# A language-model tower on one core: two rank-eight products per tile moved into two 32-row strips of the matmul array

## The chip, the cores and the metric

The kernel runs on one core of a Trainium2 chip. The time is the device time of one execution in microseconds (us), lower being better. TensorE does the matrix products (the profile calls its products PE and its weight loads PEld), VectorE is DVE, ScalarE is ACT, GpSimd is POOL and SyncE is SP.

## The reference

The input is 16 sequences of 1024 token ids. For each position the 16 latest embeddings (64 wide) are joined, multiplied by `w1` and passed through tanh; `w2` makes 1024 logits of the 64 values.

```
h = jnp.tanh(x @ w1 + b1);  logits = h @ w2 + b2
h = h + attn(layernorm(h))          # autocorrelation, top 6 lags, softmax, weighted roll
h = h + ffn(layernorm(h))           # x @ W.T + bias + sum over 16 experts of a rank-16 update
```

`attn` takes the circular autocorrelation of each row of length 1024 and adds up the row rolled by the six best lags with softmax weights; where lag 0 outweighs all others by far, it returns its input. The kernel has a short way for that case and a general one behind a flag; in the runs here the short way is taken.

## The kernel before

On the short way each output row is a sum of few matrix products of the 64 tanh values with fixed matrices. A row of `out` is `a * (product) + mean`, where `a` and `mean` are numbers per position. The product has a large part, 128 rows deep (64 rows for `h` against the centred `w2`, 64 for `beta * h` against the FFN's matrix), and a small part of rank eight: bias rows times the constants 1, beta and 1/a of each position.

Values are kept as float32r in a high and a low half. So a tile of 128 positions and 1024 outputs, in two halves `n` of 512, takes for each half three full products (`u_hi` by `w_hi`, `u_lo` by `w_hi`, `u_hi` by `w_lo`) and a fourth for the rank-eight part: `xT` by `extra`. The eight bias rows stand in `extra[i]` at partitions 32 i to 32 i + 7, with zeros elsewhere; `xT` holds the eight constants of four tiles at partitions 0, 32, 64 and 96, so the zeros of `extra[i % 4]` pick out the tile. All four products are 128 rows deep. They add up in one of the four banks of `o_ps`; two tiles fit. ScalarE evicts the first half of a tile (line 500), VectorE the second (line 676), and SP stores pairs of tiles.

A sequence has eight tiles. The work is a software pipeline over steps, one sequence per step and stage: `front` gathers the embeddings (GpSimd, `gather_rows`), transposes them and does the convolution with `w1` in two halves (lines 989 and 992); `mid` transposes the tanh values, takes moments (line 1096), computes the variances (VectorE, line 773 to 808), a chain of seven operations on GpSimd (lines 436 to 448, from `var_eps` to `beta`), and on VectorE `bh_row` in `u_rows` (line 783) and `x_row` (lines 785 to 792); `back` does the eight tile products. The orders on each engine are written out by hand. On TensorE a step is: tile 0; transposes of `h` and moments; transposes of the gathered rows; tile 1; moments; tiles 2 and 3; convolution half 0; tiles 4 and 5; a wait for `u_ready`; transposes of `u_rows` (line 1147) and, behind a wait for `x_ready`, two of `x_row` (line 1153); convolution half 1; tiles 6 and 7. ScalarE copies the transposed `x_row` to `xT` (line 574).

The rows of `extra` are made once: GpSimd fills the four tiles with zeros in step 1, behind `acf_done` (line 431), since two of them held a table before; SP then writes the eight rows into `extra[0]` (lines 344 and 347) and copies them into the other three at their partitions (line 350). TensorE waits for the first set behind step 1 and for the copies (`rows_in`) at tile 1 of step 2, the first step with tiles.

Names that the rows show: `moments` and `hbar` belong to the set-up, where lines 981 to 984 and 997 do small products with 65 rows and, at line 984, with one row (partition 64).

Of the kernel before, what the change touches and what calls it, by code (L numbers as in the profile page):

```python
# [67 lines left out]
def tower_kernel(nc, ids, wte, w1, b1, w2, b2, wT, bias, aT, bfT, coeffs, scales,  # L68
                 ident, dft, idft, acf, lags, out, force_general=False):
    ctx = ExitStack()  # L70
    with ctx:
        def sb(name, shape, dt=F32):
            return ctx.enter_context(nc.sbuf_tensor(name, shape, dt))
# [21 lines left out]
        last_moments = sb("last_moments", [P, 3])  # L95
        w_hi = sb("w_hi", [P, L], F32R)
        w_lo = sb("w_lo", [P, L], F32R)
        extra = [sb(f"extra{i}", [P, L], F32R) for i in range(4)]
        aT_sb = sb("aT_sb", [P, KC, ER])
        bfT_sb = sb("bfT_sb", [P, 2, L])  # L100
        bias_row = sb("bias_row", [1, L])
# [9 lines left out]
        hT = [sb(f"hT{p}", [P, T]) for p in range(2)]  # L111
        u_hi = [sb(f"u_hi{p}", [P, T], F32R) for p in range(2)]
        u_lo = [sb(f"u_lo{p}", [P, T], F32R) for p in range(2)]
        xT = [sb(f"xT{p}", [P, 2 * P], F32R) for p in range(2)]
        a_sb = [sb(f"a_sb{p}", [P, NT]) for p in range(2)]
        mean_sb = [sb(f"mean_sb{p}", [P, NT]) for p in range(2)]

# [3 lines left out]
        h_row = u_rows[:, 0:NT * (E + 1)].rearrange("p (i n) -> p i n", i=NT)  # L121
        bh_row = u_rows[:, NT * (E + 1):].rearrange("p (i e) -> p i e", i=NT)
        odd = sb("odd", [P, T + 1])
        x_row = sb("x_row", [P, NT, XW], F32R)
        prod = sb("prod", [P, NT, E + 1])
        quad = sb("quad", [P, NT])
        var = sb("var", [P, NT])
# [98 lines left out]
        xa_kept = sem("xa_kept")  # L226
        g_done = sem("g_done")
        w_hi_set = sem("w_hi_set")
        extra_zeroed = sem("extra_zeroed")
        w_set = sem("w_set")  # L230
        g_hi_set = sem("g_hi_set")
        row0_in, rows_in = sem("row0_in"), sem("rows_in")
# [75 lines left out]
        def _(sp):  # L308
# [29 lines left out]
            load_wT(1)  # L338
            sp.dma_start(bfT_sb[:, :, :], bfT.rearrange("(c p) n -> p c n", p=P)).then_inc(bfT_in, 16)

            sp.wait_ge(extra_zeroed, 1)
            sp.wait_ge(w_set, 3)
            for n, row in ((0, b_hi), (1, b_lo), (5, bias_hi), (6, bias_lo), (7, bias_hi)):
                sp.dma_start(extra[0][n:n + 1, :].bitcast(F32), row.bitcast(F32)).then_inc(row0_in, 16)
# [2 lines left out]
                sp.dma_start(extra[0][n:n + 1, :].bitcast(F32), row.bitcast(F32)).then_inc(row0_in, 16)  # L347
            sp.wait_ge(row0_in, 16 * NX)
            for i in range(1, 4):
                sp.dma_start(extra[i][XW * i:XW * i + NX, :].bitcast(F32), extra[0][0:NX, :].bitcast(F32)).then_inc(rows_in, 16)  # L350

            def step(g, u, front, mid, back):
                if back:
# [41 lines left out]
        def _(pool):  # L395
# [13 lines left out]
            gather(0, 0, 0)  # L409
            for i in range(NT):  # L410
                gather_rows(0, i)
            pool.memset(x_row[:, :, :].bitcast(F32), 0.0)
            pool.memset(minus_half[:, :], -0.5)
            pool.memset(g_ones[:, :], 1.0)
            pool.memset(cert_max[:, :], -3.0e38)
            pool.memset(h_row[:, :, E:E + 1], 2.0).then_inc(zeros_set, 1)
            pool.wait_ge(zeros_set, 1)
            pool.memset(x_row[:, :, 0:2].bitcast(F32), 1.0).then_inc(zeros_set, 1)

            def step(g, u, front, mid, back, last=False):  # L420
                a, b = 2 * g + u, 2 * g + u - 1
                more = front and not last
                if more:

                    gather(a + 1, 1 - u, a)
                    for i in range(NT // 2):
                        gather_rows(1 - u, i)
                if in_step(1, g, u):
                    pool.wait_ge(acf_done, 1)
                    for i in range(4):  # L430
                        last_fill = pool.memset(extra[i][:, :].bitcast(F32), 0.0)
                    last_fill.then_inc(extra_zeroed, 1)
                if mid:
                    pb = 1 - u
                    wait_alone(pool, var_ready, b + 1, pool_passed)
                    pool.tensor_scalar(var_eps[:, :], var[:, :], EPS, None, ALU.add).then_inc(scal_step, 1)  # L436
                    wait_alone(pool, scal_step, 7 * b + 1, pool_passed)
                    pool.tensor_tensor(inv_std[:, :], var_eps[:, :], minus_half[:, :], ALU.pow).then_inc(scal_step, 1)  # L438
                    wait_alone(pool, scal_step, 7 * b + 2, pool_passed)
                    pool.tensor_scalar(a_sb[pb][:, :], inv_std[:, :], 1.0, None, ALU.add).then_inc(scal_step, 1)  # L440
                    wait_alone(pool, scal_step, 7 * b + 3, pool_passed)
                    pool.tensor_tensor(a_sq[:, :], a_sb[pb][:, :], a_sb[pb][:, :], ALU.mult).then_inc(scal_step, 1)
                    wait_alone(pool, scal_step, 7 * b + 4, pool_passed)
                    pool.tensor_tensor(var2[:, :], a_sq[:, :], var[:, :], ALU.mult).then_inc(scal_step, 1)
                    wait_alone(pool, scal_step, 7 * b + 5, pool_passed)
                    pool.tensor_scalar(var2_eps[:, :], var2[:, :], EPS, None, ALU.add).then_inc(scal_step, 1)  # L446
                    wait_alone(pool, scal_step, 7 * b + 6, pool_passed)
                    pool.tensor_tensor(beta[:, :], var2_eps[:, :], minus_half[:, :], ALU.pow).then_inc(scal_step, 1)  # L448
                    if in_step(1, g, u):
                        pool.wait_ge(g_done, 1)  # L450
                    pool.wait_ge(h_ready, b + 1)
                    pool.tensor_copy(h_all[:, bass.ds(NT * E * b, NT * E)].rearrange("p (i e) -> p i e", i=NT),
                                     h_row[:, :, 0:E]).then_inc(h_saved, 1)
                if more:
                    for i in range(NT // 2, NT):
                        gather_rows(1 - u, i)
# [25 lines left out]
        def _(act):  # L482
# [20 lines left out]
            def step(g, u, front, mid, back):  # L503
# [65 lines left out]
                if mid:  # L569
                    act.wait_ge(ut_done, b + 1)  # L570
                    for odd_tiles in range(2):
                        nc.scalar.copy(tiles_of(u_hi[pb][E:P, :], odd_tiles), pair_bank(sum_ps, odd_tiles)).then_inc(hi_kept, 1)
                    act.wait_ge(xt_done, b + 1)
                    nc.scalar.copy(xT[pb][:, :], et_ps[:, 0:2 * P]).then_inc(xt_kept, 1)
                if front:
                    keep_odd(1)
                if front:
# [41 lines left out]
        def _(dve):  # L619
# [121 lines left out]
            def step(g, u, front, mid, back):  # L741
# [25 lines left out]
                def variance(hh):  # L767
# [9 lines left out]
                    dve.wait_ge(prod_ready, 2 * b + hh + 1)  # L777
                    nc.vector.tensor_reduce(in_pairs(quad[:, :])[:, pairs], products, AX.X, ALU.add).then_inc(quad_ready, 1)

                def scale_h():  # L780

                    dve.wait_ge(scal_step, 7 * b + 7)
                    nc.vector.tensor_tensor(bh_row, h_row[:, :, 0:E],  # L783
                                            beta[:, :].unsqueeze(2).to_broadcast([P, NT, E]), ALU.mult).then_inc(u_ready, 1)
                    nc.vector.reciprocal(inv_a[:, :], a_sb[pb][:, :]).then_inc(x_step, 1)
                    nc.vector.tensor_copy(x_row[:, :, 2:4], beta[:, :].unsqueeze(2).to_broadcast([P, NT, 2])).then_inc(x_step, 1)
                    dve.wait_ge(x_step, 3 * b + 1)
                    nc.vector.tensor_copy(x_row[:, :, 5:7], inv_a[:, :].unsqueeze(2).to_broadcast([P, NT, 2])).then_inc(x_step, 1)
                    dve.wait_ge(x_step, 3 * b + 2)
                    nc.vector.tensor_tensor(x_row[:, :, 4], beta[:, :], x_row[:, :, 2].bitcast(F32), ALU.subtract)  # L790
                    dve.wait_ge(x_step, 3 * b + 3)
                    nc.vector.tensor_tensor(x_row[:, :, 7], inv_a[:, :], x_row[:, :, 5].bitcast(F32),
                                            ALU.subtract).then_inc(x_ready, 1)

                if back:
# [167 lines left out]
        def _(pe):  # L963
# [78 lines left out]
            def step(g, u, front, mid, back):  # L1042
# [3 lines left out]
                def tile_product(i):  # L1046

                    if i == 0:
                        pe.wait_ge(h_hi_kept, c + 1)
                        pe.wait_ge(h_lo_kept, c + 1)  # L1050
                        pe.wait_ge(hi_kept, 2 * c + 2)
                        pe.wait_ge(lo_kept, 2 * c + 2)
                        pe.wait_ge(xt_kept, c + 1)
                    if i == 1 and in_step(2, g, u):
                        pe.wait_ge(rows_in, 48)

                    ge(pe, oa_kept, NT * c + i - 1)
                    ge(pe, ov_kept, NT * c + i - 1)
                    cols = slice(P * i, P * (i + 1))
                    factors = ((u_hi[u][:, cols], w_hi), (u_lo[u][:, cols], w_hi), (u_hi[u][:, cols], w_lo),  # L1060
                               (xT[u][:, P * (i // 4):P * (i // 4 + 1)], extra[i % 4]))
                    for n in range(2):
                        for f, (lhsT, rhs) in enumerate(factors):
                            last = mm(o_ps[:, 2 * (i % 2) + n, :], lhsT, rhs[:, 512 * n:512 * (n + 1)],  # L1064
                                      start=(f == 0), stop=(f == len(factors) - 1))
                    last.then_inc(o_done, 1)

                def transpose_rows():
# [75 lines left out]
                if mid:  # L1144
                    pe.wait_ge(u_ready, b + 1)
                    for j in range(NT // 2):
                        last = tr(sum_ps[:, P * j:P * (j + 1)], bh_row[:, 2 * j:2 * j + 2, :].rearrange("p i e -> p (i e)"),  # L1147
                                  ident_sb[:, :])
                    last.then_inc(ut_done, 1)
                    pe.wait_ge(x_ready, b + 1)  # L1150
                    ge(pe, et_lo_kept, 2 * (a + front))
                    for hh in range(2):
                        last = tr(et_ps[:, P * hh:P * (hh + 1)],
                                  x_row[:, 4 * hh:4 * hh + 4, :].bitcast(F32).rearrange("p i x -> p (i x)"), ident_sb[:, :])
                    last.then_inc(xt_done, 1)
                if front:
                    conv_half(1)
# [138 lines left out]
```

## Time and profile before

| | |
|---|---|
| time, median of 3 runs | 428.76 us (427.09 to 428.93) |
| profiled execution: span from first to last instruction | 440.3 us |
| TensorE products, busy | 409.3 us in 1886 instructions |
| TensorE weight loads, busy | 318.6 us |
| VectorE, ScalarE, GpSimd busy | 282.6, 239.9, 229.5 us |
| mean granted TensorE clock | 0.992 of full |

The profile gives the profiled execution's span and no other time of it; the span is longer than the median of the runs. In the rows, times are from the span's start. A TensorE row reads "start, length, engine, line, operation, output, inputs, rows*columns of the stationary operand, partitions x elements, count". Lengths of matmuls are modelled and overlap; starts are what to read.

### The profile page before, as it was taken

How to read it: one execution, taken by the hardware profiler on the slowest of the kernel's cores; microseconds unless marked ns; L12 is line 12 of the kernel's file. 1: busy time of each engine (PE TensorE's matmuls, PEld its weight loads, DVE VectorE, ACT ScalarE, POOL GpSimd, SP SyncE). 2: the span in 40 equal slices, each digit the busy share in tenths (PEclk: the TensorE clock that was granted, in tenths of full speed). 3: DMA queues.
4: the chain of work that ended last, by engine and by line, in shares of the span. 5: the costliest groups of instructions: out<-in, count | busy, mean ns of one | idle time of the engine just before them, and what ended most of it. 6: DMA issues, size and time to landing. Idle time of an engine off the chain costs nothing.

```text
span 440.3 us, 6477 instructions
## 1 busy us (share of the span) xinstructions
PE 409.3 (93%) x1886; PEld 318.6 (72%) x1886; DVE 282.6 (64%) x606; ACT 239.9 (54%) x359; POOL 229.5 (52%) x287
## 2 busy tenths in 40 slices
PE   2589969999999999999999999999999999999793
PEld 2465347888878777787878787878778878888582
DVE  3614866668585857677766758485857666775742
ACT  2215035666565656565656666565657556664632
POOL 6752383837566573737473847556465827131300
PEclk9999999999999999999999999999999999999998
DMA  5586002545545546354553544644636445454565
GB/s 99 186 266 255 1 16 67 218 143 222 185 192 208 199 154 247 116 223 176 189 210 125 228 165 194 211 191 172 233 110 263 145 190 209 163 218 175 207 253 228
DMA packets 27685, 79.86 MB, mean 181 GB/s; under 512 B 6187, under 2 KB 7483, under 8 KB 27669
## 3 DMA queue, kind: packets, MB, share of 16 engines
q1 hardware_dynamic: 23572, 75.46, 44.7%
q0 software_dynamic: 4096, 4.20, 4.9%
q8 instruction: 8, 0.13, 0.1%
q14 instruction: 9, 0.07, 0.0%
HBM read 12.40 MB, written 67.12 MB: 181 GB/s over the span
## 4 chain that ended last, share of the span: by engine, by line
PE 63%; POOL 13%; DVE 12%; issue 7%; ACT 2%; POOLq 1%; DMA 1%; another core or an unknown queue 1%; SPq 0%; DVEq 0%; ACTq 0%
PE o_ps L1064 35%; PE conv_ps L989 10%; PE conv_ps L992 5%; POOL beta L448 4%; POOL inv_std L438 4%; PE mix_ps L1096 2%; DVE u_rows L783 2%; DVE obuf L676 2%; PE sum_ps L1147 2%; PE sum_ps L1084 2%; DVE et_hl L754 2%; PE et_ps L1074 1%; DVE prod L773 1%; POOL var_eps L446 1%; POOL var_eps L436 1%
## 5 line engine op out<-in xcount | busy, mean ns | idle before, releaser
L500 ACT ACTIVATE obuf<-o_ps,mean_sb,a_sb 128x512 f32<-128x512 f32 x128 | 99.7, 779 | 98.4 <-PE o_ps L1064 83.4
L403 POOL DMA_INDIRECT gathered<-in_wte,idx_now x128 | 128.7, 1006 | 44.1 <-issue 34.9
L676 DVE TENSOR_SCALAR obuf<-o_ps,a_sb,mean_sb 128x512 f32<-128x512 f32 x128 | 102.6, 807 | 53.1 <-PE o_ps L1064 37.9
L1064 PE MATMUL o_ps<-w_hi,u_hi 128*128 128x512 f32 x256 | 104.8, 409 | 3.4 <-DVE obuf L676 2.5
L1064 PE MATMUL o_ps<-w_lo,u_hi 128*128 128x512 f32 x256 | 101.2, 395 | 0.0
L1064 PE MATMUL o_ps<-w_hi,u_lo 128*128 128x512 f32 x256 | 101.1, 395 | 0.0
L1064 PE MATMUL o_ps<-extra,xT 128*128 128x512 f32 x256 | 101.0, 394 | 0.0
L989 PE MATMUL conv_ps<-et_hl,shift_hi 128*128 128x512 f32 (+1 forms) x264 | 70.3, 409 | 5.1 <-DVE hT L764 2.8
L436 POOL TENSOR_SCALAR var_eps<-var 128x8 f32<-128x8 f32 x16 | 8.0, 501 | 110.1 <-DVE var L808 102.8
L989 PEld LDWEIGHTS conv_ps<-et_hl,shift_hi 128*128 128x128 f32 x264 | 50.2, 198 | 16.0 <-DVE hT L764 3.0
L1064 PEld LDWEIGHTS o_ps<-w_hi,u_hi 128*128 128x128 f32 x256 | 48.2, 188 | 17.8 <-issue 6.2
L1064 PEld LDWEIGHTS o_ps<-extra,xT 128*128 128x128 f32 x256 | 48.0, 188 | 11.7
L1064 PEld LDWEIGHTS o_ps<-w_lo,u_hi 128*128 128x128 f32 x256 | 48.1, 188 | 11.7
L1064 PEld LDWEIGHTS o_ps<-w_hi,u_lo 128*128 128x128 f32 x256 | 48.3, 189 | 9.8
L764 DVE TENSOR_TENSOR hT<-conv_ps,odd 64x512 f32<-64x512 f32 x32 | 21.9, 684 | 35.1 <-ACT odd L523 32.2
L523 ACT COPY odd<-conv_ps 64x512 f32<-64x512 f32 (+1 forms) x32 | 18.7, 584 | 35.8 <-PE conv_ps L992 33.5
L992 PE MATMUL conv_ps<-et_hh,shift_lo 128*128 128x512 f32 (+1 forms) x132 | 36.9, 401 | 0.0
L528 ACT ACTIVATE hT<-hT,b_col 64x512 f32<-64x512 f32 x32 | 22.9, 716 | 16.6 <-DVE hT L764 15.9
L448 POOL TENSOR_TENSOR beta<-var_eps,minus_half 128x8 f32<-128x8 f32 x16 | 30.5, 1909 | 2.3 <-POOL var_eps L446 1.8
L992 PEld LDWEIGHTS conv_ps<-et_hh,shift_lo 128*128 128x128 f32 x132 | 25.7, 198 | 5.9
L438 POOL TENSOR_TENSOR inv_std<-var_eps,minus_half 128x8 f32<-128x8 f32 x16 | 27.7, 1734 | 2.3 <-POOL var_eps L436 1.8
L510 ACT CAST et_hl<-et_ps 64x512 fp32r<-64x512 f32 x32 | 18.6, 582 | 15.3 <-PE et_ps L1074 14.8
(133 smaller groups left out, 443.9 us busy)
## 6 DMA issues: line engine op xcount, KB each, us to landing
out<-obuf SPq DMA_DIRECT2D x63, 1024.0 KB, 4.0
h_all<-in_wT SPq DMA_DIRECT2D x4, 1024.0 KB, 9.9
gathered<-in_wte,idx_now POOLq DMA_INDIRECT x128
aT_sb<-in_aT SPq DMA_DIRECT2D x1, 1024.0 KB
bfT_sb<-in_bfT SPq DMA_DIRECT2D x1, 1024.0 KB, 13.6
obuf<-in_w SPq DMA_DIRECT2D x2, 256.0 KB
extra<-xbar_twice SPq DMA_DIRECT2D x1, 512.0 KB
out<-obuf SPq DMA_DIRECT2D x1, 512.0 KB
```

Source lines behind the costliest of these rows:

```text
L403: pool.indirect_dma_start(gathered[p][:, i, :], None, wte, bass.IndirectOffsetOnAxis(ap=idx_now[p][:, i:i + 1].bitcast(U32), axis=0),).the ...
L438: pool.tensor_tensor(inv_std[:, :], var_eps[:, :], minus_half[:, :], ALU.pow).then_inc(scal_step, 1)
L448: pool.tensor_tensor(beta[:, :], var2_eps[:, :], minus_half[:, :], ALU.pow).then_inc(scal_step, 1)
L500: nc.scalar.activation(obuf[:, q, i % 2, 0:512], o_ps[:, 2 * (i % 2), :], ACT.Identity, bias=mean_sb[pc][:, i:i + 1], scale=a_sb[pc][:, i: ...
L510: nc.scalar.copy(tiles_of(et_hl[u][0:E, PAD:SPAN], odd_tiles), pair_bank(et_ps, odd_tiles)).then_inc(et_hi_kept, 1)
L523: nc.scalar.copy(odd[0:E, HALF * hh + 1:HALF * hh + 1 + n], conv_ps[E:P, 0:n]).then_inc(odd_kept, 1)
L528: nc.scalar.activation(hT[u][rows, 0:HALF], hT[u][rows, 0:HALF], ACT.Tanh, bias=b1_col[rows, 0:1]).then_inc(tanh_done, 1)
L676: nc.vector.tensor_scalar(obuf[:, q, i % 2, 512:L], o_ps[:, 2 * (i % 2) + 1, :], a_sb[pc][:, i:i + 1], mean_sb[pc][:, i:i + 1], ALU.mult, ...
L764: nc.vector.tensor_tensor(hT[u][E * hh:E * hh + E, 0:HALF], conv_ps[0:E, :], odd[0:E, cols], ALU.add).then_inc(shifts_added, 1)
L989: mm(conv_ps[:, 0:width], shift_hi[:, 2 * m:2 * m + 2, :], et_hl[u][:, col - 2 * m:col - 2 * m + width], start=(m == 0), stop=False)
L992: last = mm(conv_ps[:, 0:width], shift_lo[:, 2 * m:2 * m + 2, :], et_hh[u][:, col - 2 * m:col - 2 * m + width], start=False, stop=(m == J ...
L1064: last = mm(o_ps[:, 2 * (i % 2) + n, :], lhsT, rhs[:, 512 * n:512 * (n + 1)], start=(f == 0), stop=(f == len(factors) - 1))
```

## The change

The rank-eight products leave the loop over the factors. A tile now issues its six full products for both halves, and then the two rank-eight ones, each with operands of eight rows only: half `n` of tile `i` takes partitions 32 k to 32 k + 7 with k = 2 (i mod 2) + n, so the two products of a tile lie in two different 32-row strips of the array and write to two different banks. To allow it, `x_row` holds the eight constants of each tile twice (once per strip), so four transposes instead of two fill 512 columns of `xT` instead of 256; and all four copies of the bias rows stand in one `extra` tile. Nothing multiplies the zeros any more, so the zero fills and their semaphore go. The wait for the row copies moves from tile 1 to tile 0, behind the six full products.

```diff
-        extra = [sb(f"extra{i}", [P, L], F32R) for i in range(4)]
+        extra = [sb(f"extra{i}", [P, L], F32R) for i in range(2)]
-        xT = [sb(f"xT{p}", [P, 2 * P], F32R) for p in range(2)]
+        xT = [sb(f"xT{p}", [P, NT // 2 * P], F32R) for p in range(2)]
-        x_row = sb("x_row", [P, NT, XW], F32R)
+        x_row = sb("x_row", [P, NT, 2, XW], F32R)
...
-            sp.wait_ge(extra_zeroed, 1)
+            sp.wait_ge(acf_done, 1)
...
-                sp.dma_start(extra[i][XW * i:XW * i + NX, :].bitcast(F32), extra[0][0:NX, :].bitcast(F32)).then_inc(rows_in, 16)
+                sp.dma_start(extra[0][XW * i:XW * i + NX, :].bitcast(F32), extra[0][0:NX, :].bitcast(F32)).then_inc(rows_in, 16)
...
-                if in_step(1, g, u):
-                    pool.wait_ge(acf_done, 1)
-                    for i in range(4):
-                        last_fill = pool.memset(extra[i][:, :].bitcast(F32), 0.0)
-                    last_fill.then_inc(extra_zeroed, 1)
...
-                    nc.scalar.copy(xT[pb][:, :], et_ps[:, 0:2 * P]).then_inc(xt_kept, 1)
+                    nc.scalar.copy(xT[pb][:, :], et_ps[:, :]).then_inc(xt_kept, 1)
...
-                    nc.vector.tensor_copy(x_row[:, :, 2:4], beta[:, :].unsqueeze(2).to_broadcast([P, NT, 2])).then_inc(x_step, 1)
+                    nc.vector.tensor_copy(x_row[:, :, :, 2:4], both(beta).unsqueeze(3).to_broadcast([P, NT, 2, 2])).then_inc(x_step, 1)
...
-                    if i == 1 and in_step(2, g, u):
-                        pe.wait_ge(rows_in, 48)
...
-                    factors = ((u_hi[u][:, cols], w_hi), (u_lo[u][:, cols], w_hi), (u_hi[u][:, cols], w_lo),
-                               (xT[u][:, P * (i // 4):P * (i // 4 + 1)], extra[i % 4]))
+                    factors = ((u_hi[u][:, cols], w_hi), (u_lo[u][:, cols], w_hi), (u_hi[u][:, cols], w_lo))
                     for n in range(2):
                         for f, (lhsT, rhs) in enumerate(factors):
-                            last = mm(o_ps[:, 2 * (i % 2) + n, :], lhsT, rhs[:, 512 * n:512 * (n + 1)],
-                                      start=(f == 0), stop=(f == len(factors) - 1))
+                            mm(o_ps[:, 2 * (i % 2) + n, :], lhsT, rhs[:, 512 * n:512 * (n + 1)], start=(f == 0), stop=False)
+                    if i == 0 and in_step(2, g, u):
+                        pe.wait_ge(rows_in, 48)
+                    for n in range(2):
+                        k = 2 * (i % 2) + n
+                        rows = slice(XW * k, XW * k + NX)
+                        last = mm(o_ps[:, k, :], xT[u][rows, P * (i // 2):P * (i // 2 + 1)],
+                                  extra[0][rows, 512 * n:512 * (n + 1)], start=False, stop=True)
                     last.then_inc(o_done, 1)
...
-                    for hh in range(2):
-                        last = tr(et_ps[:, P * hh:P * (hh + 1)],
-                                  x_row[:, 4 * hh:4 * hh + 4, :].bitcast(F32).rearrange("p i x -> p (i x)"), ident_sb[:, :])
+                    for q in range(NT // 2):
+                        last = tr(et_ps[:, P * q:P * (q + 1)],
+                                  x_row[:, 2 * q:2 * q + 2, :, :].bitcast(F32).rearrange("p i d x -> p (i d x)"), ident_sb[:, :])
```

## Rows read from the trace of the kernel before

**Rows 1.** The page's first part: busy time, share of the span, instructions.
```profile
PE 409.3 (93%) x1886; PEld 318.6 (72%) x1886; DVE 282.6 (64%) x606; ACT 239.9 (54%) x359; POOL 229.5 (52%) x287
```

**Rows 2.** The page's fourth part: the chain that ended last, by engine.
```profile
PE 63%; POOL 13%; DVE 12%; issue 7%; ACT 2%; POOLq 1%; DMA 1%; another core or an unknown queue 1%; SPq 0%; DVEq 0%; ACTq 0%
```

**Rows 3.** Timeline of TensorE, tiles 6, 7, 0 and what follows.
```profile
229.47 0.39 PE L1064 MATMUL o_ps<-w_hi,u_hi 128*128 128x512 f32 x1
...
235.07 0.60 PE L1084 MATMUL sum_ps<-ident_sb,hT 128*128 128x128 f32 x4
235.50 0.62 PE L1096 MATMUL mix_ps<-moments_two,hT 128*128 128x134 f32 x4
```

**Rows 4.** The chain that ended last, one step: start, length, what.
```profile
211.93 1.59 PE mix_ps L1096 x4
...
224.66 1.09 DVE u_rows L783
...
225.79 0.66 PE sum_ps L1147 x4
```

**Rows 5.** Waits: who waited for whom, total, times, longest.
```profile
PE sum_ps L1147 <- DVE u_rows L783: 2.4, 10, 0.7
```

**Rows 6.** Timelines of products and weight loads in the set-up, one instruction per row.
```profile
15.37 0.35 PE L983 MATMUL o_ps<-moments,hbar 65*128 65x1 f32 x1
15.65 0.37 PE L984 MATMUL o_ps<-moments,hbar 1*128 1x3 f32 x1
...
15.88 0.35 PE L984 MATMUL o_ps<-moments,hbar 1*128 1x3 f32 x1
16.16 0.37 PE L997 MATMUL o_ps<-ident_sb,hbar 65*128 65x65 f32 x1
...
15.30 0.34 PEld L983 LDWEIGHTS o_ps<-moments,hbar 65*128 65x128 f32 x1
15.65 0.28 PEld L984 LDWEIGHTS o_ps<-moments,hbar 1*128 1x128 f32 x1
...
16.16 0.18 PEld L997 LDWEIGHTS o_ps<-ident_sb,hbar 65*128 65x128 f32 x1
```

**Rows 7.** Timeline of TensorE where 65 rows follow 128 rows.
```profile
34.22 0.39 PE L992 MATMUL conv_ps<-et_hh,shift_lo 128*128 128x512 f32 x1
34.45 0.28 PE L1167 MATMUL mix_ps<-ident_sb,obuf 65*128 65x65 f32 x2
```

**Rows 8.** Timelines of products and weight loads around a pause near the end.
```profile
410.83 0.40 PE L1064 MATMUL o_ps<-extra,xT 128*128 128x512 f32 x1
412.80 0.48 PE L1064 MATMUL o_ps<-w_hi,u_hi 128*128 128x512 f32 x1 [1.57 <-DVE obuf L676]
...
412.77 0.19 PEld L1064 LDWEIGHTS o_ps<-w_hi,u_hi 128*128 128x128 f32 x1 [1.98 <-ACT obuf L500]
412.88 0.19 PEld L1064 LDWEIGHTS o_ps<-w_hi,u_lo 128*128 128x128 f32 x1
```

**Rows 9.** Groups of instructions by line: ScalarE's copy of xT.
```profile
L574 ACT CAST xT<-et_ps 128x256 fp32r<-128x256 f32 x16 | 6.0, 373 | 0.4
```

**Rows 10.** Timelines of SP's queue and of TensorE before the first tile.
```profile
63.92 0.59 SPq L347 DMA_DIRECT2D extra<-u_hi  x1
66.31 2.13 SPq L350 DMA_DIRECT2D extra<-extra  x3
...
67.84 0.50 PE L1064 MATMUL o_ps<-w_hi,u_hi 128*128 128x512 f32 x1
```

**Rows 11.** Timeline of GpSimd in step 1, its fills and the variance chain.
```profile
41.44 3.63 POOL L431 MEMSET extra<- 128x1024 f32 x4 [11.21 <-PE o_ps L1039]
52.39 0.52 POOL L436 TENSOR_SCALAR var_eps<-var 128x8 f32<-128x8 f32 x1 [7.32 <-issue]
```

**Rows 12.** Timeline of TensorE, and one window: length, busy times by engine, granted clock.
```profile
63.49 2.84 PE L989 MATMUL conv_ps<-et_hl,shift_hi 128*128 128x512 f32 x8 [2.78 <-DVE hT L764]
...
65.00:66.00 1.00, 1.00 (x4) 0.81 (x3) 0.97 (x2) 0.78 (x2) 0.94 (x1) 0.50 0.19 37
```

More of the change, by code:

```diff
@@ L228, in tower_kernel @@
         w_hi_set = sem("w_hi_set")
-        extra_zeroed = sem("extra_zeroed")
         w_set = sem("w_set")
@@ L411, in _ @@
                 gather_rows(0, i)
-            pool.memset(x_row[:, :, :].bitcast(F32), 0.0)
+            pool.memset(x_row[:, :, :, :].bitcast(F32), 0.0)
             pool.memset(minus_half[:, :], -0.5)
@@ L417, in _ @@
             pool.wait_ge(zeros_set, 1)
-            pool.memset(x_row[:, :, 0:2].bitcast(F32), 1.0).then_inc(zeros_set, 1)
+            pool.memset(x_row[:, :, :, 0:2].bitcast(F32), 1.0).then_inc(zeros_set, 1)
             def step(g, u, front, mid, back, last=False):
@@ L778, in variance, with both @@
                     nc.vector.tensor_reduce(in_pairs(quad[:, :])[:, pairs], products, AX.X, ALU.add).then_inc(quad_ready, 1)
+                def both(col):
+                    return col[:, :].unsqueeze(2).to_broadcast([P, NT, 2])
                 def scale_h():
@@ L785, in scale_h @@
                     nc.vector.reciprocal(inv_a[:, :], a_sb[pb][:, :]).then_inc(x_step, 1)
-                    nc.vector.tensor_copy(x_row[:, :, 2:4], beta[:, :].unsqueeze(2).to_broadcast([P, NT, 2])).then_inc(x_step, 1)
+                    nc.vector.tensor_copy(x_row[:, :, :, 2:4], both(beta).unsqueeze(3).to_broadcast([P, NT, 2, 2])).then_inc(x_step, 1)
                     dve.wait_ge(x_step, 3 * b + 1)
-                    nc.vector.tensor_copy(x_row[:, :, 5:7], inv_a[:, :].unsqueeze(2).to_broadcast([P, NT, 2])).then_inc(x_step, 1)
+                    nc.vector.tensor_copy(x_row[:, :, :, 5:7], both(inv_a).unsqueeze(3).to_broadcast([P, NT, 2, 2])).then_inc(x_step, 1)
                     dve.wait_ge(x_step, 3 * b + 2)
-                    nc.vector.tensor_tensor(x_row[:, :, 4], beta[:, :], x_row[:, :, 2].bitcast(F32), ALU.subtract)
+                    nc.vector.tensor_tensor(x_row[:, :, :, 4], both(beta), x_row[:, :, :, 2].bitcast(F32), ALU.subtract)
                     dve.wait_ge(x_step, 3 * b + 3)
-                    nc.vector.tensor_tensor(x_row[:, :, 7], inv_a[:, :], x_row[:, :, 5].bitcast(F32),
+                    nc.vector.tensor_tensor(x_row[:, :, :, 7], both(inv_a), x_row[:, :, :, 5].bitcast(F32),
                                             ALU.subtract).then_inc(x_ready, 1)
```

## The prediction, as put down before the change was run

> **What bounds the kernel now.** I began with the busy shares on the page: TensorE is busy 93% of a span of 440.3 us [rows 1], and the chain that ended last runs through TensorE for 63% of it, with GpSimd at 13% and VectorE at 12% [rows 2]. A busy share does not tell how long a matmul holds up the next one, so I then read TensorE's timeline in the middle of the span. From the first matmul of tile 6 to the transposes behind tile 0 of the next step lie three tiles, 24 matmuls, and 235.07 - 229.47 = 5.60 us [rows 3]: 0.233 us from start to start, though each is drawn 0.39 us long. A tile of eight thus takes 1.867 us, and 128 tiles take 239 us. The last two products of each half of a tile are of the same size as the others, so the kernel pays 0.233 us for rank eight as for rank 128.
>
> Where the chain leaves TensorE I read one step of it in order of time [rows 4]. From the moment products on tile 0's side of the step it goes through VectorE (variance), GpSimd (seven small operations ending in beta), VectorE (u_rows) and back to TensorE's transposes at 225.79. Five tiles (1 to 5) lie on TensorE beside that chain and nearly fill it: TensorE waits for u_rows in 10 of 16 steps, 2.4 us in all [rows 5]. So a slower tile shows at once in the span, and a faster one shows only in part.
>
> **The change, part by part.** *(1) One shared slot, if the strips overlap.* The two rank-eight matmuls of a tile leave 2 x 0.233 us of the eight slots; in two row strips, into two banks, they can run side by side. Full overlap gives back 0.233 us per tile, none gives back nothing.
>
> *(2) The way into a 32-row strip and out of it.* Each tile now goes from six 128-row matmuls to two 32-row ones, and the next matmul is a 128-row one again: two crossings per tile, 256 in all. The trace of before has one such place: the products at 15.65 and 15.88 have one row, those before and behind have 65 [rows 6]. No wait stands between them in the code. Start to start inside the strip is 15.88 - 15.65 = 0.23 us; across the crossings it is 0.28 us both times. More telling are the weight loads: inside one kind of matmul the load starts ahead of its matmul (15.30 for 15.37), but at both crossings it starts with it (15.65, 16.16). Few rows alone do not do this: where 65 rows follow 128, the step is 34.45 - 34.22 = 0.23 us, the ordinary one [rows 7].
>
> I read this as: at a crossing the next weights are not loaded until the matmul before has left the array. These products are one to three columns wide; the kernel's have 512 columns. Serially, then, 0.28 us and the columns, at most a slot of 0.233: 0.51 us. A second way agrees: the drawn length 0.39 us [rows 3], then the exposed load. After a pause the load at 412.77 is followed by the next load at 412.88, so a load takes 0.11 us [rows 8]; 0.39 + 0.11 = 0.50. I take 0.50 us from start to start at a crossing instead of 0.233. The bound from below is the row's own 0.28, as if the columns hid the rest; that I hold unlikely, since the load cannot be hidden behind columns if it waits for them.
>
> The Trainium skill, "TensorEngine Tiling (Array Packing)", section "Key Properties", says that a change of tiling mode drains TensorE, which speaks against this change; it gives no price. The loads of [rows 6] agree with it; by the rule the sum below holds, without it one of the first two rivals does.
>
> *(3) The second strip behind the first.* No row shows two strips at once. Bounds: together (0), and a full slot later (0.233). I take 0.11, one weight load behind the other, as both loads come at the crossing and a load takes 0.11 [rows 8]. The skill's "TensorE: Matmul & The Clock Gate", Part 3, gives matmuls in different row strips starts some 4 ns apart; by that the sum below would be about 13 us lower (an estimate from that page). No run here shows it yet.
>
> Per tile: five full slots, 5 x 0.233 = 1.167; crossing 0.50; second strip 0.11; crossing 0.50: 2.277 us against 1.867, **+0.41 us**. Over 128 tiles +52.5 us.
>
> *(4) x_row and xT.* Four transposes instead of two per sequence: a transpose takes (235.50 - 235.07)/4 = 0.108 us [rows 3], so 2 x 0.108 x 16 = +3.5 us on TensorE. The four VectorE operations on x_row write twice the elements; they run behind u_rows while TensorE transposes, and add under 0.1 us per step. ScalarE's copy of xT (0.373 us for 256 columns [rows 9]) doubles its columns; it ends long before the next tile 0 asks for it, behind a convolution half and tiles 6 and 7. Without that cover both would cost up to 0.5 us x 16 = 8 us.
>
> *(5) The wait for the strip rows.* It moves from tile 1 to behind tile 0's six products, once. The rows are copied by SP: its wait for the first set passes at 66.31, 2.4 us after the last issue at 63.92, and the three copies take 2.13 us to issue [rows 10]. The last begins its issue at about two thirds of that, 67.8, and by the same 2.4 us lands near 70.2. Tile 0 starts at 67.84 [rows 10], its six products end near 69.3: TensorE, with all behind it, waits 0.9 us. Call it +0.8.
>
> *(6) The four fills of GpSimd go.* They take 3.63 us from 41.44, and the variance chain starts only at 52.39, after 7.32 us in which nothing that the profile shows held GpSimd [rows 11]. The fills end at 45.07. If that pause stays, the chain begins some 0.7 us earlier; if it goes with the fills, up to those 7.3 us could come back. I take -0.7. SP's wait for the fills becomes one for the correlation, long past when w_set opens: nothing.
>
> *(7) Pauses that a slower tile fills.* The waits for u_rows (2.4 us [rows 5], with the reload 3.0) go, as five tiles beside the chain grow by 2.05 us. Near the end TensorE stands from 410.83 + 0.233 to 412.80 [rows 8], 1.74 us, behind the last such chain, which the slower tiles fill too; for the last wait for u_lo I put one tile's growth, 0.4: together -2.2.
>
> Sum: 52.5 + 3.5 + 0.8 - 0.7 - 3.0 - 2.2 = **+50.9 us**, on the profiled span 440.3 to 491. The span is 11.5 us above the median of the runs shown, 428.76, and the profile does not say where; I add the same microseconds to the median: 479.7, in proportion 478.3. I say **479 us**.
>
> **Rivals.**
> *Gain: no drain.* The strips load in the background and run side by side, as the packing table in Part 3 of the skill's "TensorE: Matmul & The Clock Gate" has it. Then a tile is 0.233 us shorter. In the 10 steps that hang on the chain of rows 4 only tiles 6, 7 and 0 count: 3 x 0.233 - 0.216 = 0.48 us each, 4.8. The five others lie between that and 8 x 0.233 - 0.216 = 1.65, say 1.07: 5.4. The last eight tiles give 1.9. Together -12: 417 us. It decides as soon as both crossings and the second strip together cost under 0.233 us per tile. Against it: the two loads in rows 6 that did not run ahead. Chance 0.11.
>
> *Loads exposed, no drain.* A load waits for the columns of the matmul before but not for its end: each crossing costs 0.233 + 0.11. The tile is 1.167 + 0.343 + 0.11 + 0.343 = 1.963, +0.096; 12.3 us, and with the other terms (less absorbed) 12: 441 us. For it: 0.28 against 0.23 is a small step. Against it: that step was seen with hardly any columns to wait for. Chance 0.11.
>
> *The clock falls.* With gaps inside every tile the granted clock could go from its upper level (2.4 GHz) to its lower one (1.2 GHz), as it did (0.50 at 65 to 66 us) after TensorE had stood 2.78 us [rows 12]. Six slots twice as long add 1.4 us per tile, over 600 us. The gaps here are a few tenths each and the clock held through shorter waits. Chance 0.04.
>
> **How the numbers follow.** Forecast (drain at every crossing): 0.74. Its own range: second strip together, +0.30 per tile, 38.4 - 1.6 = 36.8, 465; a full slot behind, +0.53, 68.2 - 1.6 = 66.6, 495. Reaching to the exposed-load case at 441, the range is 437 to 500. The gain case and the clock case, 0.15, and a little of the tails stay out. A change of 0.5% (2.1 us) is about what a measurement of this kernel tells from none. Faster: the gain case, with the low bound of the crossings, 0.12. Same: 0.03, where the costs happen to cancel. Slower: 0.85.
>
> **What would show it.** In the profile after: the start of the first strip matmul some 0.5 us after the start of the sixth product, its weight load not ahead of it; the second strip's start about 0.11 us behind; the next tile's first product 0.5 us behind that; a tile of 2.28 us; the steps some 3.3 us longer; no wait of TensorE for u_rows; a clock at its upper level. The forecast is wrong if the strip's weight load lies under the sixth product, or if the next tile's load lies under the strips.

## The result and the profile after

The change makes the kernel slower: 446.17 us (median of 4 runs, 445.55 to 447.25) against 427.92 (426.44 to 428.93), a ratio of 1.041 with a 95% interval of 1.036 to 1.046. The forecast was 479 with a range of 437 to 500: the direction and the mechanism came out, but +18 us instead of +51.

The page after, the lines that answer to [rows 1, 2]: span, busy times, chain by engine.

```profile
span 443.4 us, 6537 instructions
...
PE 423.7 (96%) x1918; PEld 288.9 (65%) x1918; DVE 280.2 (63%) x606; ACT 243.3 (55%) x359; POOL 219.2 (49%) x283
...
PE 92%; DVE 3%; DMA 2%; ACT 1%; SPq 1%; issue 1%; ACTq 0%
```

TensorE is now nearly the whole chain, and no wait for u_rows is left. The mean granted clock is 0.996, its upper level.

TensorE's timeline after, products and then weight loads, over the end of tile 6, tile 7 and the begin of the next step; the stretch answers to [rows 3].

```profile
227.85 0.51 PE L1059 MATMUL o_ps<-w_hi,u_hi 128*128 128x512 f32 x1
...
229.12 0.40 PE L1059 MATMUL o_ps<-w_lo,u_hi 128*128 128x512 f32 x1
229.45 0.50 PE L1065 MATMUL o_ps<-extra,xT 8*128 8x512 f32 x2
229.88 0.50 PE L1059 MATMUL o_ps<-w_hi,u_hi 128*128 128x512 f32 x1
230.22 0.39 PE L1059 MATMUL o_ps<-w_hi,u_lo 128*128 128x512 f32 x1
...
231.91 0.66 PE L1085 MATMUL sum_ps<-ident_sb,hT 128*128 128x128 f32 x4
...
247.05 0.60 PE L1154 MATMUL et_ps<-ident_sb,x_row 128*128 128x128 f32 x4
247.41 2.10 PE L987 MATMUL conv_ps<-et_hl,shift_hi 128*128 128x512 f32 x8
...
256.26 0.66 PE L1085 MATMUL sum_ps<-ident_sb,hT 128*128 128x128 f32 x4
...
229.45 0.18 PEld L1065 LDWEIGHTS o_ps<-extra,xT 8*128 8x128 f32 x2 [0.36 <-issue]
229.88 0.19 PEld L1059 LDWEIGHTS o_ps<-w_hi,u_hi 128*128 128x128 f32 x1 [0.24 <-issue]
229.99 0.19 PEld L1059 LDWEIGHTS o_ps<-w_hi,u_lo 128*128 128x128 f32 x1
```

A tile takes 229.88 - 227.85 = 2.03 us, 0.163 more than before and 0.247 less than the 2.277 forecast. Both strips stand in one line of two (x2), at one start, and so do their two loads: there is no lag. No load runs ahead at a crossing, here or anywhere else where TensorE goes straight on: in recorded starts the way in is 0.32 or 0.33 us at 127 of 128 tiles and the way out 0.42 or 0.43 at 125 of 127, the others being waits. Where a load is exposed, the product's recorded start is that of its load: the product at 229.88 is followed at 230.22, 0.34 later, while the next load starts at 229.99 and its product a slot later. I read this as feeding that starts 0.11 us, one load, behind such a start. From feed to feed the way into the strips takes 229.45 + 0.11 - 229.12 = 0.44 us and the way out 229.99 - 229.56 = 0.43, each in place of a slot of 0.233.

### The profile page after: what moved, and what is told of

Same layout as the page of the kernel before. It is cut to its first block, busy times and chain, and to the rows that moved or that the text cites. A ratio compares the mean times of both kernels' runs of the same rounds, so it can differ in the third digit from the quotient of the medians.

```text
span 443.4 us, 6537 instructions
## 1 busy us (share of the span) xinstructions
PE 423.7 (96%) x1918; PEld 288.9 (65%) x1918; DVE 280.2 (63%) x606; ACT 243.3 (55%) x359; POOL 219.2 (49%) x283
## 4 chain that ended last, share of the span: by engine, by line
PE 92%; DVE 3%; DMA 2%; ACT 1%; SPq 1%; issue 1%; ACTq 0%
PE o_ps L1059 42%; PE conv_ps L987 14%; PE o_ps L1065 12%; PE conv_ps L990 7%; PE o_ps L1021 3%; PE sum_ps L1097 2%; PE sum_ps L1085 2%; PE sum_ps L1148 2%; PE mix_ps L1097 2%; PE et_ps L1075 1%; PE et_ps L1154 1%; PE sum_ps L1011 1%; PE o_ps L1027 1%; DMA w2c<-in_b 1%; DMA extra<-extra 1%
## 5 line engine op out<-in xcount | busy, mean ns | idle before, releaser
L402 POOL DMA_INDIRECT gathered<-in_wte,idx_now x128 | 124.5, 972 | 44.6 <-issue 34.9
L1059 PE MATMUL o_ps<-w_hi,u_hi 128*128 128x512 f32 x256 | 110.8, 433 | 1.7 <-DVE obuf L670 1.3
L987 PE MATMUL conv_ps<-et_hl,shift_hi 128*128 128x512 f32 (+1 forms) x264 | 71.3, 412 | 0.8 <-DVE hT L758 0.5
L1065 PE MATMUL o_ps<-extra,xT 8*128 8x512 f32 x256 | 64.0, 496 | 0.6 <-DMA extra<-extra 0.6
L987 PEld LDWEIGHTS conv_ps<-et_hl,shift_hi 128*128 128x128 f32 x264 | 48.8, 197 | 13.7 <-issue 4.0
L1065 PEld LDWEIGHTS o_ps<-extra,xT 8*128 8x128 f32 x256 | 23.6, 181 | 47.4 <-issue 46.3
L517 ACT COPY odd<-conv_ps 64x512 f32<-64x512 f32 (+1 forms) x32 | 18.7, 584 | 34.4 <-PE conv_ps L990 34.4
L442 POOL TENSOR_TENSOR beta<-var_eps,minus_half 128x8 f32<-128x8 f32 x16 | 27.6, 1726 | 2.3 <-POOL var_eps L440 1.8
L851 DVE TENSOR_TENSOR u_lo<-sum_ps,u_hi 64x512 fp32r<-64x512 f32 x32 | 22.1, 689 | 9.7 <-ACT u_hi L566 9.0
```

The costliest lines, as they stand in the source:

```text
L402: pool.indirect_dma_start(gathered[p][:, i, :], None, wte, bass.IndirectOffsetOnAxis(ap=idx_now[p][:, i:i + 1].bitcast(U32), axis=0),).the ...
L851: nc.vector.tensor_tensor(tiles_of(u_lo[pb][E:P, :], odd_tiles), pair_bank(sum_ps, odd_tiles), tiles_of(u_hi[pb][E:P, :], odd_tiles).bitca ...
L987: mm(conv_ps[:, 0:width], shift_hi[:, 2 * m:2 * m + 2, :], et_hl[u][:, col - 2 * m:col - 2 * m + width], start=(m == 0), stop=False)
L1065: last = mm(o_ps[:, k, :], xT[u][rows, P * (i // 2):P * (i // 2 + 1)], extra[0][rows, 512 * n:512 * (n + 1)], start=False, stop=True)
```

## The experiments

**Before, looked at again.**

> The kernel before, unchanged, for a second profile. The profiled execution that the prediction was built on had a span of 440.3 us, while its runs take 427.9 and the changed kernel's time is 2.2 us above its span (445.55 against 443.4). Theory: that execution was a slow one, by pauses beside the tiles (GpSimd's 7.3 us pause behind the fills, the waits for u_rows); then the span here is near 426 us, first tile well before 67.8 us, tile still 1.867 us. Rival: the profile of before is typical and times and spans stand apart in this kernel; then the span is near 440 us again.

Measured: 427.75 us. From the page (span), then the timeline of TensorE:

```profile
span 425.6 us, 6477 instructions
...
61.04 0.47 PE L1064 MATMUL o_ps<-w_hi,u_hi 128*128 128x512 f32 x1
...
201.88 0.60 PE L1084 MATMUL sum_ps<-ident_sb,hT 128*128 128x128 f32 x4
...
215.79 0.60 PE L1147 MATMUL sum_ps<-ident_sb,u_rows 128*128 128x128 f32 x4
216.23 0.41 PE L1153 MATMUL et_ps<-ident_sb,x_row 128*128 128x128 f32 x2
216.39 2.09 PE L989 MATMUL conv_ps<-et_hl,shift_hi 128*128 128x512 f32 x8
...
224.86 0.60 PE L1084 MATMUL sum_ps<-ident_sb,hT 128*128 128x128 f32 x4
```

The execution that the prediction was made from was some 15 us longer than this one (440.3): 6.8 of them lie ahead of the first tile (67.84 there), most of the others in nine steps of 23.5 to 23.8 us. Sizes below are taken against this one. Here TensorE does not wait for u_rows at all, a step takes 22.98 us, and the first tile starts at 61.04. After the change a step takes 256.26 - 231.91 = 24.35: +1.37 per step, 19.2 over the 14 whole steps between the first tile 0 and the last, with the first tile 2.2 us earlier (below): 17.0 of the 17.8 us between the spans. The step's own parts are 8 x 0.163 = 1.30 and 0.20 for the transposes (0.36 from x_row to convolution, against 0.16), 1.50. Of the 0.13 between them, 0.12 lies where the way out leads into transposes, behind tiles 5 and 0. There a load was exposed in part before the change too: four transposes take 0.49 us instead of 0.44 (246.56 to 247.05 after, 215.79 to 216.23 before), so the strips add 0.05 there and not 0.11.

**All of the change but the strips.** The last two products of a tile run over all 128 rows; the terms of two tiles, each twice, are added to every tile.

```diff
-                        rows = slice(XW * k, XW * k + NX)
+                        rows = slice(0, P)
```

> The changed kernel with the two last products of a tile taken over all 128 rows again (they then add up the rank-eight terms of two tiles twice, so the output is another one); order, transposes of x_row, no fills, all as in the changed kernel. Theory (the loss is the crossings into and out of the 32-row strips, 0.40 us per tile, less one shared slot of 0.233): tile 1.867 us, 128 x 0.163 = 20.9 us less than the changed kernel, about 425 us. Rival (the order of the products or the four transposes cost the time): 440 us or more.

Measured: 429.87 against 429.59, ratio 1.001 (0.998 to 1.004). TensorE's timeline, the last two products of two tiles in a row:

```profile
213.19 0.62 PE L1065 MATMUL o_ps<-extra,xT 128*128 128x512 f32 x2
...
215.05 0.64 PE L1065 MATMUL o_ps<-extra,xT 128*128 128x512 f32 x2
```

The tile is back at 1.86 us. The order, the doubled x_row and xT, the moved wait and the missing fills together come to nothing that can be told from noise; all of the loss is in the strips.

**Both halves in one strip.** The second product then has to follow the first.

```diff
-                        rows = slice(XW * k, XW * k + NX)
+                        rows = slice(XW * 2 * (i % 2), XW * 2 * (i % 2) + NX)
```

> The changed kernel with both halves' rank-eight products in the same 32-row strip. Theory (in two strips they run side by side, start to start near 0): a full slot more, tile 2.03 + 0.23 = 2.26 us, 128 x 0.23 = 30 us more than the changed kernel, about 476 us. Rival (in two strips they run one after another already, and the crossings cost only 0.17 us together): no difference, 446 us. The forecast's lag of 0.11 us: tile 2.15, 461 us.

Measured: 475.4, ratio 1.106 (1.100 to 1.111). TensorE's timeline, sixth product, strip pair, next tile:

```profile
232.91 0.40 PE L1059 MATMUL o_ps<-w_lo,u_hi 128*128 128x512 f32 x1
233.24 0.73 PE L1065 MATMUL o_ps<-extra,xT 8*128 8x512 f32 x2
233.90 0.50 PE L1059 MATMUL o_ps<-w_hi,u_hi 128*128 128x512 f32 x1
```

From the strips to the next product 0.66 us instead of 0.43: a slot more. In two strips, then, the products do run side by side. That 475.4 is near the 479 that I had forecast for the change is accident: the forecast had the second strip 0.11 behind, not a slot.

**Half the columns in the strips.** The rank-eight part of the other 256 columns of each half is left out.

```diff
-                        last = mm(o_ps[:, k, :], xT[u][rows, P * (i // 2):P * (i // 2 + 1)],
-                                  extra[0][rows, 512 * n:512 * (n + 1)], start=False, stop=True)
+                        last = mm(o_ps[:, k, 0:256], xT[u][rows, P * (i // 2):P * (i // 2 + 1)],
+                                  extra[0][rows, 512 * n:512 * n + 256], start=False, stop=True)
```

> The changed kernel with strip products over 256 of the 512 columns of each half (the rank-eight part of the other 256 is left out). Theory (at a crossing the next weights load when the columns of the product before are through and the array is empty, so the strip's columns stand in full between the two crossings): the way from strip to the next full product is 0.107 us shorter, 128 x 0.107 = 14 us less than the changed kernel, about 433 us. Rival (a fixed price of 0.43 us per change of mode, columns hidden in it): 447 us, no difference to the changed kernel.

Measured: 433.17, ratio 1.009 (1.006 to 1.012). TensorE's timeline, the same three places:

```profile
200.98 0.39 PE L1059 MATMUL o_ps<-w_lo,u_hi 128*128 128x512 f32 x1
201.30 0.38 PE L1065 MATMUL o_ps<-extra,xT 8*128 8x256 f32 x2
201.61 0.50 PE L1059 MATMUL o_ps<-w_hi,u_hi 128*128 128x512 f32 x1
```

The way out falls from 0.43 to 0.31: the next 128-row product does wait for the strips' columns, 256 of them being worth 0.12 us and 512 about a slot. The crossing of 0.44 is then about 0.23 of columns, 0.11 of load, and some 0.10 that neither accounts for, in which, as I read it, the array is empty.

**The fills put back.** The change with the four zero fills and SP's wait for them.

```diff
...
-            sp.wait_ge(acf_done, 1)
+            sp.wait_ge(extra_zeroed, 1)
...
+                if in_step(1, g, u):
+                    pool.wait_ge(acf_done, 1)
+                    for i in range(4):
+                        last_fill = pool.memset(extra[i][:, :].bitcast(F32), 0.0)
+                    last_fill.then_inc(extra_zeroed, 1)
```

> The changed kernel with GpSimd's four zero fills and the wait for them put back. Theory (the fills delayed the variance chain of step 1, and the first tile with it; the changed kernel starts it 2.2 us earlier than the second profile of before): 2 us more than the changed kernel, about 448 us, first tile near 61 us. Rival (nothing in the set-up hangs on them): 446 us, first tile near 58.8. The forecast's bound of 7.3 us: 453 us.

Measured: 450.7, ratio 1.048 (1.045 to 1.051), against 1.041 without them. Timelines of GpSimd and of TensorE up to the first tile, and one window (length, busy times by engine, granted clock); then the same timelines of the changed kernel:

```profile
36.83 3.63 POOL L431 MEMSET extra<- 128x1024 f32 x4 [6.75 <-PE o_ps L1043]
47.78 0.52 POOL L436 TENSOR_SCALAR var_eps<-var 128x8 f32<-128x8 f32 x1 [7.32 <-issue]
...
58.89 2.86 PE L993 MATMUL conv_ps<-et_hl,shift_hi 128*128 128x512 f32 x8 [2.56 <-DVE hT L764]
...
63.25 0.48 PE L1065 MATMUL o_ps<-w_hi,u_hi 128*128 128x512 f32 x1
...
62.00:63.00 1.00, 1.00 (x4) 0.81 (x3) 0.00 (x0) 0.00 (x0) 0.70 (x2) 0.50 0.37 53
```

```profile
41.41 0.26 POOL L430 TENSOR_SCALAR var_eps<-var 128x8 f32<-128x8 f32 x1 [11.84 <-issue]
...
55.82 2.12 PE L987 MATMUL conv_ps<-et_hl,shift_hi 128*128 128x512 f32 x8 [0.52 <-DVE hT L758]
...
58.83 0.47 PE L1059 MATMUL o_ps<-w_hi,u_hi 128*128 128x512 f32 x1
```

The pause of some 7 us behind the fills comes back with them. It is not `var` that is late: VectorE's last write to it runs from 39.51 for 0.97 us here. In the changed kernel GpSimd stands even longer at this place, 11.84 us, but there it waits for `var`, which is written until 39.78, and `var_eps` starts 1.6 us later. The trace holds two more instructions of GpSimd, named `MODIFY_POOL_CONFIG`, which the views leave out. With the fills they stand at 40.47 and 40.51, right behind the last fill, and `var_eps` starts 7.27 us after the second. In the changed kernel they stand at 29.64 and 29.68, right behind the gathers, so that most of what follows them lies under the wait for `var`. The pause thus seems to belong to these instructions, and the fills to put it off until nothing covers it. No run here takes the instructions out, so this is not shown, nor how long the pause is by itself.

The first tile starts 4.42 us later with the fills. Of this 1.35 is TensorE's clock: convolution half 1 takes 63.25 - 58.89 = 4.36 us instead of 58.83 - 55.82 = 3.01, at a granted clock of 0.50, its lower level (1.2 GHz), after TensorE had stood 2.56 us. In the second look at the kernel before it had stood as long at this place, and the clock held at 1.00. The other 3.1 us agree with the ratios, by which the fills were worth about 3 us (0.007 x 428); by the medians it is 4.5. Neither is the 0.7 of the forecast.

**Halves of 64 rows.** Operands of 40 rows at partition 0 or 64, one in each half of the rows; terms of other positions are added.

```diff
-                        rows = slice(XW * k, XW * k + NX)
+                        rows = slice(64 * n, 64 * n + XW + NX)
```

> The changed kernel with its last two products over 40 rows each, partitions 0 to 39 and 64 to 103, so they take two halves of 64 rows of the array in place of two strips of 32 (they add up rank-eight terms of other positions too, so the output is another one). Theory (every change of the rows that a product takes up, 128 to fewer and back, is paid alike): the tile stays 2.03 us, 446 us. Rival (only the 32-row strips cost a crossing): two products side by side without crossings, 7 slots, 1.63 us per tile, some 400 to 412 us, as far as the chain to u_rows lets it. Rival (64-row halves do not run side by side): 2.26 us, 475 us.

Measured: 447.02, ratio 1.041 (1.035 to 1.046): as the change itself. TensorE's timeline:

```profile
230.21 0.39 PE L1059 MATMUL o_ps<-w_lo,u_hi 128*128 128x512 f32 x1
230.53 0.49 PE L1065 MATMUL o_ps<-extra,xT 40*128 40x512 f32 x2
230.95 0.50 PE L1059 MATMUL o_ps<-w_hi,u_hi 128*128 128x512 f32 x1
```

0.32 in and 0.42 out, the two products again at one start: the price hangs on leaving the 128-row form and is the same for 40 rows as for 8.

**No rank-eight products.** They are left out altogether.

```diff
...
-                        last = mm(o_ps[:, k, :], xT[u][rows, P * (i // 2):P * (i // 2 + 1)],
-                                  extra[0][rows, 512 * n:512 * (n + 1)], start=False, stop=True)
```

> The changed kernel without its rank-eight products (that part of the output is left out; x_row, its transposes and xT are still made). It shows how far a shorter tile is worth anything. TensorE alone: a tile of 1.40 us, 0.63 less, 446 - 128 x 0.63 = 366 us. With the chain from the moments through VectorE and GpSimd to u_rows (some 13 us per step, as the four-strip run shows) and 8.3 us behind it: 21.4 us per step, about 400 us.

Measured: 409.95, ratio 0.953 (0.950 to 0.957). TensorE alone would have fallen by some 60 us (256 slots of 0.233); 20 came. In the waits (who waited for whom, total, times, longest) TensorE now stands in front of u_rows in 14 steps:

```profile
PE sum_ps L1143 <- DVE u_rows L781: 15.4, 14, 1.2
```

So even free strips could not have given 5%, unless the chain to u_rows finds other work beside it.

**Four strips at one visit.** Since a visit pays two crossings however many strips it has, the strips of two tiles go together behind the even tile's six products; the odd tile's banks are opened by them.

```diff
+                    first = i % 2 == 0
...
+                    if first:
...
+                        for j in (i, i + 1):
+                            if j > i:
+                                ge(pe, oa_kept, NT * c + i)
+                                ge(pe, ov_kept, NT * c + i)
+                            for n in range(2):
+                                k = 2 * (j % 2) + n
+                                rows = slice(XW * k, XW * k + NX)
+                                strip = mm(o_ps[:, k, :], xT[u][rows, P * (i // 2):P * (i // 2 + 1)],
+                                           extra[0][rows, 512 * n:512 * (n + 1)], start=(j > i), stop=(j == i))
```

> The strip products of two tiles issued together, behind the first tile's six full products: four strips, four banks, half the crossings (the second tile's banks are opened by its strip products). Theory (crossings 0.40 per visit, strips side by side): two tiles in 12 x 0.233 + 0.40 + 0.233 = 3.43 us against 4.06 in the changed kernel and 3.73 before; TensorE alone would give 446 - 64 x 0.63 = 406 us, the chain from the moments over GpSimd to u_rows holds it near 22.2 us per step, so 412 to 416 us, faster than both kernels. Rival (strips one after another, cheap crossings): two tiles in 3.89 us, 435 us.

Measured: 423.89, ratio 0.985 (0.980 to 0.990): faster than before by one to two per cent. TensorE's timeline over two tiles, then their wait:

```profile
219.54 0.40 PE L1060 MATMUL o_ps<-w_lo,u_hi 128*128 128x512 f32 x1
219.86 0.51 PE L1072 MATMUL o_ps<-extra,xT 8*128 8x512 f32 x4
220.30 0.50 PE L1060 MATMUL o_ps<-w_hi,u_hi 128*128 128x512 f32 x1
...
223.29 0.51 PE L1072 MATMUL o_ps<-extra,xT 8*128 8x512 f32 x4
223.73 0.66 PE L1094 MATMUL sum_ps<-ident_sb,hT 128*128 128x128 f32 x4
...
237.36 0.66 PE L1157 MATMUL sum_ps<-ident_sb,u_rows 128*128 128x128 f32 x4 [0.49 <-DVE u_rows L781]
...
238.40 2.10 PE L987 MATMUL conv_ps<-et_hl,shift_hi 128*128 128x512 f32 x8
...
PE sum_ps L1157 <- DVE u_rows L781: 4.9, 10, 0.5
```

Four strips cost what two do (0.32 in, 0.44 out). Two tiles take 223.29 - 219.86 = 3.43 us against 3.73. Over 64 pairs of tiles that is 19 us; some 6.6 (1.5% of 429.6) arrive in the time. In the step of the rows, which lasts 22.89 us (from 223.73 to 246.62) against 22.98 before, most of it goes again at one place: TensorE waits 0.49 us for u_rows, as it does in 10 steps, and from those transposes to the convolution it then takes 238.40 - 237.36 = 1.04 us instead of 216.39 - 215.79 = 0.60, of which 0.20 are the two more transposes. The products are no longer what bounds this stretch; the chain to u_rows is.

**Tile 6 as cover.** In the last kernel, tile 6 is moved ahead of the wait for u_rows on TensorE, ScalarE and VectorE; and the same move alone in the kernel before.

```diff
...
-                if back and not front:
+                if back:
                     tile_product(6)
...
-                if back and front:
-                    tile_product(6)
```

> The four-strip kernel with tile 6 in every step ahead of the wait for u_rows, on TensorE, ScalarE and VectorE, so six tiles stand beside the chain from the moments to u_rows instead of five. In the four-strip run TensorE waited for u_rows and a step took 22.9 us. Theory (that chain is its bound): TensorE no longer waits, a step takes the 21.8 us of its own work, 424 - 16 x 1.1 = 406 us, at most 412. Rival (the chain only moves, since convolution half 1 and what hangs on it come later): 422 to 426 us.

> The kernel before with tile 6 ahead of the wait for u_rows in every step, and nothing else. It tells whether the gain of the four-strip kernel with this order is that of the order. Theory (in typical executions of before TensorE does not wait for u_rows, as its second profile shows, so more cover is worth nothing): 427 to 430 us, the same as before. Rival (executions of before lose time in that wait often): 2 to 4 us faster.

Measured: 419.13, ratio 0.975 (0.971 to 0.979), and for the move alone 429.03, 0.998 (0.995 to 1.001). With four strips the wait for u_rows is gone; in the kernel before there was none to cover. The 4.8 us between this kernel and the last are near the 4.9 of that wait, but part of them is TensorE's clock: two of the four executions of the last kernel had a mean granted clock of 0.987 and took 425.0 and 425.1 us, the two with 0.995 and 0.996 took 422.8 and 422.2, and those of this kernel had 0.991 to 0.997. At like clock the move is worth some 3.5 us. Less came than the 406 to 412 that I had expected. TensorE's timeline, two visits, with the weight loads of the second visit's last two strips and VectorE's eviction ahead of them:

```profile
202.25 0.72 PE L1068 MATMUL o_ps<-extra,xT 8*128 8x512 f32 x4
202.90 0.50 PE L1056 MATMUL o_ps<-w_hi,u_hi 128*128 128x512 f32 x1
...
212.10 1.03 PE L1068 MATMUL o_ps<-extra,xT 8*128 8x512 f32 x4
213.06 0.66 PE L1153 MATMUL sum_ps<-ident_sb,u_rows 128*128 128x128 f32 x4
...
212.61 0.21 PEld L1068 LDWEIGHTS o_ps<-extra,xT 8*128 8x128 f32 x2 [0.33 <-issue]
...
211.68 0.81 DVE L668 TENSOR_SCALAR obuf<-o_ps,a_sb,mean_sb 128x512 f32<-128x512 f32 x1
```

From strips to the next product it is 0.65 and 0.96 here, not 0.44. The odd tile's two strips wait for the eviction of their banks, which this order asks for earlier: at the second visit their loads start 0.51 us behind the first two, 0.12 after VectorE's eviction ends (211.68 + 0.81 = 212.49). No run takes this wait away.

## Why the prediction was right in direction and wrong in size

*Steps (2) and (3), the crossings and the lag, were mis-sized; their mechanism holds as far as the runs show it (the load stands bare and the columns are paid; what the rest of a crossing is stays a reading).* Per tile I had 0.247 us too much, 31.6 us over 128 tiles, of a miss of 32.7. By the steps, 16 x (1.37 - 0.20), the strips cost 18.7 us, where I had 52.5.

- The lag of the second strip, taken as 0.11, is 0: 14 us. The loads were thought to go one behind the other; the timeline shows both at 229.45, and one strip for both adds a slot. The Trainium skill, "TensorEngine Tiling (Array Packing)", section "Key Properties", also says that different tiles can load weights in parallel, and "TensorE: Matmul & The Clock Gate", Part 3, has matmuls in different row strips start some 4 ns apart; the trace agrees with both to its 0.01 us.
- A crossing, taken as 0.50, is 0.43 to 0.44: about 17 us over 256. Its parts are of the expected kind, the columns, an exposed load and some 0.10 more. But my two ways to 0.50 agreed by accident. One added the whole 0.28 of [rows 6], which has a load and some columns in it, to a whole slot; and it took that 0.28 from a stretch in which TensorE seems to have run at half its speed (below). The other took the drawn length 0.39 for the time in the array; the next load starts 0.33 behind.

TensorE's timeline before, behind [rows 6]:

```profile
17.29 1.12 PE L1074 MATMUL et_ps<-ident_sb,gathered 128*128 128x128 f32 x4 [0.76 <-DVE moments_two L658]
...
23.89 3.58 PE L989 MATMUL conv_ps<-et_hl,shift_hi 128*128 128x512 f32 x8 [2.36 <-ACT odd L547]
27.31 1.09 PE L992 MATMUL conv_ps<-et_hh,shift_lo 128*128 128x512 f32 x4
```

Eight products of 512 columns take 27.31 - 23.89 = 3.42 us here, 0.43 each and not 0.233, like those at a granted clock of 0.50 in the run with the fills (0.43 each, four from 61.55 to 63.25). Four transposes are drawn over 1.12 us, where they take 0.60 in the steps. The profile gives a granted clock of 1.00 for this stretch and for [rows 6], which these lengths speak against. The prediction did not reckon with it. What the crossing of [rows 6] would cost at the upper level no run shows.

*Step (1)*, the shared slot, holds: side by side, as the one-strip run shows. *Step (4)*: 0.20 per step for the transposes, 3.2 us (forecast 3.5); the copies hid. *Step (5)*: the rows come late by 0.6 us (forecast 0.8). *Step (6)* was small where it should have been near the middle of its bounds, about -3 instead of -0.7: without the fills most of the pause lies under the wait for `var`. *Step (7)* was mostly empty: the waits for u_rows, worth -3.0 in the forecast, belong to the longer execution and were not there to be filled in the second look. Near the end the two waits went from 1.57 and 0.71 to 1.32 and 0.38, -0.6 instead of -2.2. Steps (4) to (7) come to +0.3 us together in the run without strips (429.87 against 429.59); the forecast had -1.6.

*The rivals.* No drain is out: no load runs ahead, in any run with strips. "Loads exposed, no drain" came nearer in time (441), but by its lag of 0.11, which is not there; without it its tile would be 1.167 + 2 x 0.343 = 1.853, under the 1.867 of before, and the measured 2.03 has 0.09 more at each crossing. That I read as the time in which the array runs empty. In the changed kernel the clock stayed at its upper level. The measured 446 lies in the stated range only because I had stretched this down to that rival; the forecast's own range was 465 to 495.

## What to carry to other kernels

A change between 128-row matmuls and row strips costs about 0.20 us each way over the ordinary slot (512 columns, 0.44 instead of 0.233), so a visit must save more than 0.40 us: two strips share one slot and lose 0.17 per tile, four share three and win 0.30 per pair of tiles. Gather strips at one visit before you use them, and then look at the next bound: here the chain to u_rows took back much of the gain until one more tile covered it, which brought 423.9 down to 419.1 us, some 3.5 of it at like clock. Look at more than one execution before you put a price on its pauses: those of 2.4 us that I had absorbed were not in the next one. And before you take a price from a few rows of a set-up, see at what speed a known product runs beside them.

## What the runs showed of the hardware that I had not expected

- The weight loads of two and of four strips start at one recorded time (each 0.18 us long), and four strips cost as much as two (0.44 us to the next product).
- The drawn end of a matmul is too late for this: the array takes the next load 0.33 us behind the start of a product drawn 0.39 us long.
- Products of 40 rows, one in each 64-row half, cost the same crossings as those of 8 rows in 32-row strips (447.02 and 446.17 us).
- GpSimd starts nothing for 6.85 to 7.27 us behind a `MODIFY_POOL_CONFIG` that follows four fills of 3.63 us in total, in the four runs that have them; in the eight runs without, the same instruction stands 10.9 to 12.2 us ahead of the next operation, for the most part under the wait for `var`. That the pause is its own is likely and not shown.
